# A five-layer message-passing kernel: the ends of its eight phases rearranged, sums zeroed by ScalarE, the source score made by VectorE

## What is computed

```python
L0: agg = segment_sum(edge_vals[:, None] * x[edge_src], edge_dst);  agg @ W.T + b
L1, five times:
    W = ssp(rbf @ fw1[i] + fb1[i]) @ fw2[i] + fb2[i];  W = W * C[:, None]
    agg = segment_sum((x @ lin1_w[i])[src] * W, dst) / denom
    x = x + ssp(agg) @ lin2_w[i] + lin2_b[i];  x = layernorm(x) * ln_g[i] + ln_b[i]
L2: alpha = tanh(s_dst[dst] + s_src[src] + gate_b);  z = segment_sum(h[src] * (alpha * d[dst] * d[src] * w)[:, None], dst)
L3: agg = segment_sum(feat[edge_src], edge_dst);  agg @ W.T + b
```

## Time and profile before

| | us |
|---|---|
| median of three runs | 4603.52 (4602.52 to 4611.04) |
| the profiled execution | 4598.03 |
| its span, first to last instruction | 4596.2 |
| POOL busy | 3302.7 |

### The profile page before, as it was taken

One profiled execution on the slowest core, in us unless ns is written; L12 is line 12 of the kernel. 1 busy time (PEld: TensorE's weight loads), 2 busy tenths in 40 slices (PEclk: granted clock), 3 DMA queues, 4 the chain that ended last, 5 costly groups with the idle time before them and its releaser, 6 DMA issues. The chain is left out here.

```text
span 4596.2 us, 51942 instructions
## 1 busy us (share of the span) xinstructions
PE 2524.6 (55%) x13213; PEld 2251.8 (49%) x13213; DVE 2082.9 (45%) x4555; ACT 1837.8 (40%) x4373; POOL 3302.7 (72%) x3337
## 2 busy tenths in 40 slices
PE   3454456666566665666556665566663333333333
PEld 2444456655455554555555554566662333323333
DVE  4222255554555546555555555555553344421111
ACT  2112146665565645565456564555551111100000
POOL 5777767776777767777677776777753777767776
PEclk9999987776677766777667776766665555555555
DMA  6333222222222212222222222222211222212222
GB/s 136 90 98 96 71 58 68 70 69 51 64 68 67 69 47 68 68 69 67 55 62 67 68 67 55 60 65 67 64 42 30 55 57 56 57 43 56 55 56 53
DMA packets 194095, 297.28 MB, mean 65 GB/s; under 512 B 81758, under 2 KB 116680, under 8 KB 193788
## 3 DMA queue, kind: packets, MB, share of 16 engines
q0 software_dynamic: 106496, 219.17, 19.1%
q10 hardware_dynamic: 33942, 57.75, 4.4%
q1 hardware_dynamic: 53350, 16.87, 1.5%
HBM read 271.98 MB, written 21.57 MB: 64 GB/s over the span
## 5 line engine op out<-in xcount | busy, mean ns | idle before, releaser
L576 POOL DMA_INDIRECT rows<-table,staged_src x3328 | 3301.7, 992 | 1280.1 <-issue 888.9
L727 PE MATMUL pD<-scatter,msg 128*128 128x80 f32 x4160 | 774.9, 364 | 716.8 <-PEq L725 710.8
L727 PEld LDWEIGHTS pD<-scatter,msg 128*128 128x128 f32 x4160 | 733.2, 273 | 786.0 <-issue 786.0
L666 PE MATMUL pD<-scatter,rows 128*128 128x80 f32 x2496 | 573.0, 424 | 887.7 <-PEq L664 540.1
L666 PEld LDWEIGHTS pD<-scatter,rows 128*128 128x128 f32 x2496 | 544.1, 330 | 919.0 <-issue 919.0
L714 PE MATMUL pC<-fw,hidden 128*128 (+1 forms) x4160 | 809.9, 370 | 187.7 <-PEq L712 185.3
L714 PEld LDWEIGHTS pC<-fw,hidden 128*128 128x128 f32 x4160 | 755.3, 278 | 222.5 <-issue 221.5
L894 ACT ACTIVATE scatter<-onehot,c_e 128x80 f32<-128x80 bf16 x2080 | 549.5, 346 | 484.2 <-ACTq L892 483.6
L1226 DVE TENSOR_TENSOR msg<-msg,rows 128x512 f32<-128x512 f32 x520 | 336.4, 688 | 646.1 <-DVEq L1034 629.5
L1030 DVE COPY staged_src<-src_i 128x8 int32<-128x8 int32 x416 | 74.3, 179 | 727.5 <-DVEq L1038 727.5
L876 ACT ACTIVATE hidden<-hidden 128x512 f32<-128x512 f32 x520 | 327.5, 630 | 62.3 <-ACTq L779 1.6
(11 more groups left out here) (190 smaller groups left out, 1570.4 us busy)
## 6 DMA issues: line engine op xcount, KB each, us to landing
rows<-table,staged_src POOLq DMA_INDIRECT x3328
basis<-basis_d ACTq DMA_DIRECT2D x130, 256.0 KB, 2.8
table<-node_rows SPq DMA_DIRECT2D x66, 128.0 KB
msg<-in_edge_weight_dram ACTq DMA_DIRECT2D x54, 128.0 KB, 3.0
basis_d<-basis ACTq DMA_DIRECT2D x26, 256.0 KB, 3.6
hidden<-in_edge_weight_dram ACTq DMA_DIRECT2D x48, 128.0 KB, 3.3
out_dram<-node_rows SPq DMA_DIRECT2D x12, 128.0 KB
table<-node_rows SPq DMA_DIRECT2D x11, 132.0 KB
```

The lines of the kernel that those rows point to most:

```text
L576: pool.indirect_dma_start(out=rows[:, s, j, 0:width], out_offset=None, in_=tab[:, :], in_offset=bass.IndirectOffsetOnAxis(ap=staged_src[:, ...
L666: mm = pe.matmul(sum_ps, rows[:, g % RING, j, 0:D], scatter[:, g % 2, j, :], start=(j == 0), stop=(j == CH - 1))
L727: mm = pe.matmul(sum_ps, msg_of(g, h)[:, c * D:(c + 1) * D], scatter[:, g % 2, HALF * h + c, :], start=(h == 0 and c == 0), stop=(h == 1 a ...
```

## The change

- The node tiles are laid out anew: 22 whole tiles from the front, then three whole tiles counted back from the end, so that tile 22 covers 75 nodes again that tile 21 has. The last block is one tile (`END`), ahead of it stand two of two tiles (`MID`, complete after group 50, and `PRE`, after group 47).
- The last group of a phase is handled in two halves: its last four gathers signal a semaphore of their own, and products and sums are made for each half. `MID`'s node steps stand between the halves, and `END`'s mean comes right behind the last add.
- Fixed lags of the node steps are replaced by an order written out by engine. In the conv loop VectorE does later steps of older blocks first and the mean last, TensorE does turn and scores in one place, five groups after the mean. In the first, gated and counting phases a block's steps all stand in the group after it is complete.
- The source score is a product with a broadcast weight and a reduction on VectorE (`gate_rows`), instead of narrow matmuls and a ScalarE step; the gate's bias goes into the destination score.
- `agg` is zeroed by ScalarE at the end of a phase's own steps (`zero_sums`); VectorE waits for it in `start_sums`. Before the first phase it is still a memset.
- The first table is written in seven DMAs instead of five, and one more weight is loaded (the source half of the gate, for all partitions).
- SP stores blocks where their rows are made; the last three after the second half's relay, `MID` in two DMAs that leave out the nodes seen before.

The diff, cut to its core (SP; POOL; TensorE; ScalarE; VectorE):

```diff
-TAIL = N_NODES - (TILES - 1) * P
+WHOLE = N_NODES // P - 2
+TILE_AT = tuple(t * P if t < WHOLE else N_NODES - (TILES - t) * P for t in range(TILES))
+SEEN = WHOLE * P - TILE_AT[WHOLE]
...
-BLOCK_TILES = tuple((t, t + 1) for t in range(0, TILES - 3, 2)) + ((TILES - 3, TILES - 2, TILES - 1),)
+BLOCK_TILES = tuple((t, t + 1) for t in range(0, TILES - 1, 2)) + ((TILES - 1,),)
 BLOCKS = len(BLOCK_TILES)
+PRE, MID, END = BLOCKS - 3, BLOCKS - 2, BLOCKS - 1
 LATE_EDGES = 600
-NODE_STEPS = 8
+BLOCK_END = tuple(TILE_AT[ts[-1]] + P for ts in BLOCK_TILES)
+DONE_AT = tuple(min(GROUPS, -(-(N_EDGES // N_NODES * end + LATE_EDGES) // GROUP)) - 1 for end in BLOCK_END)
+MEAN_AT = tuple(d + d % 2 if b < PRE else d for b, d in enumerate(DONE_AT))
...
+                        for g in range(GROUPS):
+                            relay(n, p, g)
+                            for b in range(PRE):
+                                if store_at(b) == g:
+                                    store(b, tensor)
+                        relay_last(n, p)
+                        for b in range(BLOCKS):
+                            if b >= PRE or store_at(b) >= GROUPS:
+                                store(b, tensor)
...
+                def after_edges(lead):
+                    return lambda b: DONE_AT[b] + lead
+
+                def after_mean(b):
+                    return MEAN_AT[b] + 5
...
+                                ).then_inc(gathers[s] if g < GROUPS - 1 or j < HALF else gathers_last, 16)
...
                 def first_edges():
                     with pe.Fori(0, n_pass):
-                        for g in range(GROUPS + NODE_STEPS):
-                            if g < GROUPS:
-                                plain_sums(g, degrees=True)
-                            for b in due(g, 1):
+                        for g in range(GROUPS + 1):
+                            if g == GROUPS - 1:
+                                sums_may_start(g)
+                                degrees(g)
+                            for b in done(g - 1):
                                 node_linear(b, w0T[:, :])
-                            for b in due(g, 3):
                                 node_turn(b, y[:, block_tiles(b), :], relu_full)
-                            for b in due(g, 4):
+                                if g == GROUPS - 1:
+                                    rows_in(g)
+                                    row_sums(g, 0, HALF)
                                 node_table(b, lin1[:, 0, :])
+                            if g < GROUPS - 1:
+                                sums_may_start(g)
+                                degrees(g)
+                                rows_in(g)
+                                row_sums(g, 0, CH)
+                            if g == GROUPS - 1:
+                                last_rows_in()
+                                row_sums(g, HALF, CH)
 
...
+                            for b in done(g - 1):
                                 node_linear(b, None)
+                            if g < GROUPS - 1:
+                                sums_may_start(g)
+                                row_sums(g, 0, CH)
+                            if g == GROUPS - 1:
+                                sums_may_start(g)
+                                row_sums(g, 0, HALF)
+                                pe.wait_ge(scatter_full, 1)
+                                pe.sem_inc(scatter_full, -1)
+                                row_sums(g, HALF, CH)
...
                             if last:
-                                for b in due(g - 6, 0, even=True):
+                                for b in conv_due(g - 5):
+                                    node_turn(b, node_h[:, :, :], u_full)
                                     node_scores(b)
...
+                        g = GROUPS - 1
+                        sums_may_start(g)
+                        message_sums(g, 0)
+                        node_lin2(MID, l)
+                        if not last:
+                            node_turn(MID, u[:, block_tiles(MID), :], u_full)
+                            message_sums(g, 1)
+                            node_table(MID, lin1[:, l + 1, :])
+                            node_lin2(END, l)
+                            node_turn(END, u[:, block_tiles(END), :], u_full)
+                            node_table(END, lin1[:, l + 1, :])
+                        else:
+                            node_turn(PRE, node_h[:, :, :], u_full, filt_ps[0])
+                            node_scores(PRE, filt_ps[1])
+                            message_sums(g, 1)
+                            node_lin2(END, l)
+                            for b in (MID, END):
+                                node_turn(b, node_h[:, :, :], u_full, filt_ps[0])
+                                node_scores(b, filt_ps[1])
...
+                def zero_sums():
+
+                    act.activation(agg[:, :], ones[:, 0:1].broadcast_to([P, NPAD + WIN]), ACT.Copy, scale=0.0).then_inc(agg_zero, 1)
...
+                        node_log_of(MID)
+                        if not last:
+                            node_turned(MID)
+                            node_guess(MID)
+                            node_log_of(END)
+                            node_turned(END)
+                            node_guess(END)
+                        else:
+                            node_turned(PRE, filt_ps[0])
+                            node_scores(PRE, filt_ps[1])
+                            node_guess(MID)
+                            node_log_of(END)
+                            node_relu(MID, node_h[:, :, :], x)
+                            node_guess(MID)
+                            node_guess(END)
+                            node_turned(MID, filt_ps[0])
+                            node_scores(MID, filt_ps[1])
+                            node_relu(END, node_h[:, :, :], x)
+                            node_guess(END)
+                            node_turned(END, filt_ps[0])
+                            node_scores(END, filt_ps[1])
+                    zero_sums()
...
+                            for part in (slice(0, CH),) if g < GROUPS - 1 else (slice(0, HALF), slice(HALF, CH)):
+                                act.wait_ge(gate_in, 1)
+                                act.sem_inc(gate_in, -1)
+                                act.activation(gate[:, g % 2, part, :], gate[:, g % 2, part, :], ACT.Tanh).then_inc(gate_full, 1)
+                                if part.start == 0:
+                                    for b in done(g - 1):
+                                        node_relu(b, node_h[:, :, :], x2)
+                                        node_guess(b)
+                        else:
+                            node_relu(END, node_h[:, :, :], x2)
+                            node_guess(END)
+                zero_sums()
...
                 def start_sums():
-                    dve.memset(agg[:, :], 0.0)
+                    dve.wait_ge(agg_zero, 1)
+                    dve.sem_inc(agg_zero, -1)
+                    start_windows()
+
+                def start_windows():
...
+                        for g in range(GROUPS - 1):
+                            rows_in(g)
+                            gate_halves(g, slice(0, CH), True)
+                            for b in done(g - 1):
+                                gated_block(b)
+                        g = GROUPS - 1
+                        rows_in(g)
+                        gate_halves(g, slice(0, HALF), True)
+                        gated_block(MID)
+                        last_rows_in()
+                        gate_halves(g, slice(HALF, CH), False)
+                        add_sums(g, rows_read=True)
+                        dve.sem_inc(agg_full, 1)
...
                     part = node_h[:, 0:size(b), :]
                     own(dve.tensor_tensor(part, part, of_tiles(rstd, b), ALU.mult))
-                    dve.tensor_tensor(node_rows[:, b % 2, 0:size(b), 0:D], part, of_tiles(dcol, b), ALU.mult).then_inc(u_full, 1)
+                    dve.sem_inc(u_full, 1)
+                    dot, new = node_dot[:, 0:size(b), :], node_rows[:, b % 2, 0:size(b), :]
+                    own(dve.tensor_tensor(dot, part, over_tiles(w_src[:, :], size(b)), ALU.mult))
+                    dve.tensor_tensor(new[:, :, 0:D], part, of_tiles(dcol, b), ALU.mult)
+                    own(dve.tensor_reduce(new[:, :, D:D + 1], dot, AX, ALU.add))
+                    dve.sem_inc(tab_full, 1)
 
...
+                            if g == GROUPS - 2:
+                                node_deviation(PRE)
                                 if last:
-                                    conv_out(b)
-                            if last:
-                                for b in due(g - 4, 0, even=True):
+                                    conv_out(PRE)
+                                else:
+                                    conv_rows(PRE, l)
+                            add_sums(g)
```

(51 more changed lines are left out.)

394 lines of the change are left out of this document (192 added, 202 removed).

## The result

The changed kernel takes 4560.84 us (median of 4 runs, 4553.41 to 4565.09), the kernel before beside it 4603.34: ratio 0.9902, 95% interval 0.9885 to 0.992. That is 42.5 us less where 79.6 were forecast, outside the range and beyond rival B's 4544. The profiled executions, 4598.03 before and 4563.3 after (span 4561.5), differ by 34.7; all that follows is booked against those.

What follows compares the result with a forecast made beforehand. POOL's gathers and its idle time at phase ends were taken to bound the kernel; the terms 0.4 - 3.4 - 31.6 - 31 + 1.6 - 3.6 - 12 = -79.6 us, from 4603.5, gave 4524 us, range 4490 to 4554.

Steps and rivals of the forecast that it cites:

- rival B: Last conv phase: the stall only changes its engine, VectorE's added steps help eat the 7.2, lag stays; 4544 us, chance 15%.
- Plain ends: Ends of the four plain conv phases: halves and a one-tile last block save 7.9 us each, 31.6 in all.
- first end: End of the first phase: last add 1.7 us later, then one tile and no older rows save 5.1; net -3.4.
- last end: End of the last phase: half the sums, one-tile linear, smaller add and one store fewer; -3.6 us.
- Zeroing: Starts of seven phases: without VectorE's memset the gathers beside it get shorter; -12 us in all.
- Rival C: Phase starts: no zeroing gain, as a memset neighbour or the first product on y holds the gather; 4536 us, chance 7%.
- The last conv phase: Its end: lag behind gathers falls 20 us over nine blocks, the last block's chain 11; together 31 us saved.
- ScalarE gets 7.2 back: Last conv phase, each block: turn and score stand in one group, so ScalarE's 7.23 us wait before the score copy goes.
- The tail: Last conv phase's end: the last block's chain of 40.5 us was to shrink by 10.9, with the store 11.
- The term of 7.6 for blocks in series: Last conv phase's end: two blocks of output and rows in series on VectorE add 7.6 us.
- The gated end: Gated phase's end: the middle block's chain between the halves delays the last add; net +1.6 us, ends -1 and +4.
- rival A: Last conv phase keeps pace, TensorE granted 2.4 GHz in more groups, all 48.3 us of lag can go; 4496 us, chance 13%.

Runs made afterwards that it cites:

- the memset run: The changed kernel with the sums zeroed on VectorE by a memset again, ScalarE's zeroing and the wait for it taken out: 4575.03 us, ratio 0.9935.
- the fastest kernel of all: Changed kernel with four reorderings: first phase's blocks behind sums, gated window read before wait, relu and turned copy moved, middle block behind second half: 4522.43 us, ratio 0.9804.

## Why the prediction was right or wrong

**What bounds the kernel: right.** But for the 3.8 us after the last gather, what was gained or lost lies in POOL's gathers or in its idle time ahead of phases.

**Plain ends, first end, last end: right.** 28.0 of 31.6, 4.6 of 3.4, 3.8 of 3.6; idle of 15.9 to 16.8 was forecast near 15 (before, the four were 23.07 to 23.24).

**Zeroing: right in sign and size, in part by luck.** 13.0 of 12, and 16.7 when it is undone. The rule of the Trainium skill, page "SBUF — State Buffer", section "Who interferes with whom", by which the memset would not contend with GpSimd on this generation, is not what this chip shows: a gather that starts 0.03 after the memset takes 3.80 instead of 0.94. The rule leaves out the two-port modes; whether the memset ran in one, no trace here shows. Rival C, to which that rule would lead, falls by the sum. The forecast let a product on y catch the first gather and still saved 1.7 in each of five phases. What came was uneven: in two of the five the first gather met a product and took longer than before (4.15 and 4.16 against 3.0 to 3.1), as the second half of rival C has it, and in three it met none and its next four took 3.1 to 3.4 each. Ahead of the count phase it took 3.53. So "first gathers of a phase near 1 us" came true in four of seven phases, and its opposite, "first gathers still at 3", in three. In the gated phase the memset held the second gather (3.24), not the first, whose 0.94 stands in rows 3.

**The last conv phase: wrong**, by the step "TensorE now holds the sums of that group until ScalarE has done the next block's log and the copy (2.8 more)". The engine and the place were right, but the step stopped at the sums. Behind them in TensorE's queue stand the filters and the hidden units, and it is for those that ScalarE then waits: "ScalarE gets 7.2 back" became 6.32 of a new wait in the block shown, 71.7 in the phase where 18.6 had been. That left 0.7 a cycle where the step had 2.2. The 2.8 was itself too small: TensorE stood 3.2 a block at the scores (28.8 in nine), and in the block shown 1.31 more for the score. The first product of the last group starts 41.4 us behind the last gather instead of 50.0: 8.6 gained where 20 were forecast. This is the first half of rival B, held at 15%; its second half, VectorE's two added steps, is the 3 to 4 us of the run without the source score. Moving copy and score ahead of the log took 17.6 more off this lag.
The tail fell from 40.5 to 35.3 (76.8 less 41.4), not by 11, and stays at 35.6 and 35.0 with the turned copy and the relu moved, so this miss is a separate one. The timeline of the changed kernel in it:
```profile
3421.22 0.68 DVE L1347 TENSOR_TENSOR msg<-msg,rows 128x512 f32<-128x512 f32 x1
...
3427.90 0.69 DVE L1347 TENSOR_TENSOR msg<-msg,rows 128x512 f32<-128x512 f32 x1 [0.26 <-DVEq L1144]
...
3430.35 1.96 PE L776 MATMUL pD<-scatter,msg 128*128 128x80 f32 x8 [1.00 <-PEq L774]
...
3436.05 0.24 DVE L1154 TENSOR_TENSOR agg<-agg,pD 128x80 f32 x1 [0.68 <-issue]
```
The two products start 6.7 apart, since the older block's rows and the middle block's sum stand between them, and the last add comes 3.7 after its sums, behind the middle block's output. Before, they started 0.6 apart. Halves save time where rows are still landing; here all rows had landed 40 us earlier, so the steps put between the halves only delayed the second. The term of 7.6 for blocks in series was too small, as it seems: no run has this end without the halves.

**The gated end: right in sign**, +3.0 for +1.6, inside its ends; moving the middle block gave 4.4 back.

**Gathers inside the phases: not in the sum at all.** The first paragraph called work inside a phase "free or worthless unless it shortens one of these gaps or a gather itself", and the steps then looked at gathers at phase starts alone. Two edits got no price for that: the register read that moved behind the wait (13.2 by itself) and the first phase's block steps in one go (7.8 in the profile). Against the profiles the forecast missed 44.9 us: 27.5 of them are the table's last three rows, 17.3 the last conv phase's end. The second profile of the changed kernel is 13.5 shorter; against that one the miss is 31.3, with 14.7 in the three rows and 18.4 in that end.

**TensorE's clock decided nothing, and rival A falls.** The mean granted clock is 0.695 before and 0.637 after, but 0.699 in the memset run, which is slower than its control at 0.639, and 0.698 in the fastest kernel of all. Two runs of the changed kernel at 0.700 and 0.637 took 4558.59 and 4558.15. In the last conv phase, where rival A wanted more of it, the clock was 0.69 before and 0.70 after.

**Start:** the first gather came at 39.2 to 42.4 in all profiles, so a load of 0.4 can't be seen there.

## What to carry to other kernels

When a wait is taken from one engine and put on another, follow that engine's queue past the first instruction that is held, to whoever waits for the second and third: here the gain came back to the engine it was taken from. Where one engine issues at a steady beat and another works in step with what lands, a shift of half a microsecond can make them meet in every turn, so a move that costs nothing on its own engine is to be checked against the beat. A term that is read at one place (a gather held at a phase's start) is to be looked for at all places where the same two meet. And splitting the last group into halves pays only where its rows are what the phase's end waits for.

## What the runs showed of the hardware

A gather that starts while VectorE works on two operands that both lie in SBUF (128x256 to 128x3200 elements) ends 0.82 us after the VectorE instruction does (mean, with 0.81 to 0.83 for each kind of instruction); one that has started ahead of it keeps its 0.95. It depends on where the operands lie: beside a VectorE instruction that reads one of them from PSUM (the buffers pA to pD) no gather is held. In the changed kernel's last conv phase:
```profile
3006.71 0.75 DVE L1334 SCALAR_TENSOR_TENSOR hidden<-pB,nfb_l,hidden 128x512 f32<-128x512 f32 x1 [1.32 <-DVEq L1333]
3006.83 0.94 POOL L605 DMA_INDIRECT rows<-table,staged_src  x1 [0.30 <-issue]
...
3012.38 1.28 DVE L1347 TENSOR_TENSOR msg<-msg,rows 128x512 f32<-128x512 f32 x2
3013.25 1.22 POOL L605 DMA_INDIRECT rows<-table,staged_src  x1 [0.31 <-issue]
```
The first gather starts 0.12 after its VectorE instruction and takes 0.94; the second starts beside a product of msg and rows and ends 0.81 after it. Over all thirteen profiles, of the gathers that started at least 0.06 after a VectorE instruction did and 0.2 ahead of its end, 5413 were beside two SBUF operands and all were held, 2473 beside a PSUM operand and none was. Beside the memset a gather ends 1.04 after it, which is 0.81 after the short copy of 128x416 that follows. VectorE's side does not pay: the memset takes 2.79 with a gather beside it, the one-hot 0.82 or 0.83 with or without one. ScalarE zeroes the same 128x3280 in 2.94, and gathers beside ScalarE's work keep 0.95. Reading a register from SBUF behind a wait put 0.6 us between the landing and the instruction that used it.
